# A recurrent layer stack on one core: the channel mix's output product in three passes by block pairs, the second norm by ScalarE, the numerator ahead of the mixing

## The reference, cut to what matters

```
h  = layernorm(x, ln1_w, ln1_b);  hh = time_shift(h)
xk, xv, xr = h * tm + hh * (1 - tm)            # tmk, tmv, tmr
k, v, sr = xk Wk', xv Wv', sigmoid(xr Wr')
x  = x + (sr * wkv(time_decay, time_first, k, v)) Wo'
h  = layernorm(x, ln2_w, ln2_b);  hh = time_shift(h)
xk = h * cmk + hh * (1 - cmk);  xr = h * cmr + hh * (1 - cmr)
kf = square(relu(xk Wck'))                     # 1024 hidden channels
kv = kf Wcv'                                   # "channel mix's output product"
x  = x + sigmoid(xr Wcr') * kv
```

## Time and profile before

| what | value |
|---|---|
| median of three runs | 1927.9 us (1927.41 to 1932.6) |
| the profiled execution | 1932.82 us, its span 1931.1 us |
| mean granted TensorE clock | 0.967 of full |
| TensorE matmul busy | 1812.3 us (94%) |
| TensorE weight load busy | 1536.1 us (80%) |
| VectorE busy | 1233.3 us (64%) |
| ScalarE busy | 841.0 us (44%) |
| GpSimd busy | 2.7 us (0%) |

### The profile page before, as it was taken

The page is one execution under the profiler, slowest core; times in us unless marked ns, Lnnn a source line. Parts: engine busy times, 40 slices in busy tenths (PEclk is TensorE's granted clock), DMA queues, the critical chain, the costliest instruction groups (busy, mean ns, idle before and its releaser), DMA issues. The chain is left out here.

```text
span 1931.1 us, 26354 instructions
## 1 busy us (share of the span) xinstructions
PE 1812.3 (94%) x10124; PEld 1536.1 (80%) x10124; DVE 1233.3 (64%) x1953; ACT 841.0 (44%) x1304; POOL 2.7 (0%) x24
## 2 busy tenths in 40 slices
PE   2499999999999997999899999999999999999997
PEld 1277887777887776777689998899998899998996
DVE  6889999899998844677554454454454454454445
ACT  2565776666766543333233333333333333333333
POOL 0000000000000000000000000000000000000000
PEclk9699999999999998999789999999999999999999
DMA  3000000001001003111020000000000000001001
GB/s 109 6 22 17 12 27 34 6 28 39 1 12 49 1 1 95 42 42 36 11 76 33 34 25 10 33 33 33 33 18 14 33 33 33 33 11 60 1 1 39
DMA packets 35274, 56.54 MB, mean 29 GB/s; under 512 B 3094, under 2 KB 20476, under 8 KB 34684
## 3 DMA queue, kind: packets, MB, share of 16 engines
q1 hardware_dynamic: 35196, 55.47, 8.8%
HBM read 51.79 MB, written 3.67 MB: 29 GB/s over the span
## 5 line engine op out<-in xcount | busy, mean ns | idle before, releaser
L1489 DVE TENSOR_TENSOR hf<-sil,fbanks 128x512 f32<-128x512 f32 (+1 forms) x128 | 79.4, 620 | 332.2 <-PE fbanks L1658 273.4
L1597 ACT ACTIVATE sil<-fbanks 128x512 f32<-128x512 f32 (+1 forms) x128 | 69.6, 544 | 442.2 <-PE fbanks L1658 442.2
L1674 PE MATMUL fbank<-wl,hh 128*128 128x256 f32 x896 | 250.3, 279 | 0.0
L1674 PE MATMUL fbank<-wh,hl 128*128 128x256 f32 x896 | 250.1, 279 | 0.0
L1674 PE MATMUL fbank<-wh,hh 128*128 128x256 f32 x896 | 250.1, 279 | 0.0
L715 PE MATMUL pair<-wcv,kf 128*112 128x256 f32 x768 | 176.2, 379 | 0.0
L1489 DVE TENSOR_TENSOR hf<-sil,fbank 128x512 f32<-128x512 f32 (+1 forms) x128 | 79.5, 621 | 149.7 <-PE fbank L1658 142.7
L1674 PEld LDWEIGHTS fbank<-wl,hh 128*128 128x128 f32 x896 | 168.3, 188 | 2.2
L1674 PEld LDWEIGHTS fbank<-wh,hh 128*128 128x128 f32 x896 | 168.4, 188 | 1.8
L1674 PEld LDWEIGHTS fbank<-wh,hl 128*128 128x128 f32 x896 | 168.4, 188 | 0.0
L1496 DVE TENSOR_TENSOR hl<-hf,hh 128x512 fp32r<-128x512 f32 (+1 forms) x256 | 158.2, 618 | 0.0
(11 more groups left out here) (235 smaller groups left out, 3495.1 us busy)
## 6 DMA issues: line engine op xcount, KB each, us to landing
raw<-in_w_gate SPq DMA_DIRECT2D x16, 512.0 KB, 3.8
raw<-in_w_up SPq DMA_DIRECT2D x16, 512.0 KB, 4.7
raw<-in_w_down SPq DMA_DIRECT2D x16, 512.0 KB, 5.6
raw<-in_w_ck SPq DMA_DIRECT2D x4, 1024.0 KB, 4.8
wcv<-in_w_cv SPq DMA_DIRECT2D x4, 768.0 KB, 4.4
raw<-in_ctx_t SPq DMA_DIRECT2D x4, 750.0 KB, 6.3
ct<-in_ctx_t SPq DMA_DIRECT2D x4, 750.0 KB, 5.1
x<-in_x SPq DMA_DIRECT2D x4, 448.0 KB, 6.1
```

The lines of the kernel that those rows point to most:

```text
L1489: dve.tensor_tensor(hf[i][:, 0:w], sil[i][:, 0:w], bank[2 * i + 1][:, 0:w], ALU.mult).then_inc(hf_ready, 1)
L1597: act.activation(sil[f % 2][:, 0:w], bank[2 * (f % 2)][:, 0:w], ACT.Silu).then_inc(sil_ready, 1)
L1674: ins = pe.matmul(bank[4 + 2 * (t % 2) + i // 2][:, (i % 2) * C:(i % 2 + 1) * C], a[t % 2][:, f, i * P:(i + 1) * P], m[h][:, DOWN + f * C: ...
```

## The change

1. All 8 blocks of the output product are split (`SPLIT` is gone, `FT = 8`), so it has 96 fp32r matmuls a step. The tile `wcv` and its load go; the whole of `in_w_cv` (1024 KB) passes through `stage`, and `wcvh`, `wcvl` have 2048 columns in place of 512.
2. The product runs over block pairs outside and sequences inside, so that four sums (two banks, two sums in each) stay open. TensorE does pairs 0 and 1, the transposes of norm 1, pairs 2 and 3. Each pair waits for its own `kfl_ready`; `cv_done` comes in the last pair.
3. ScalarE copies all four groups of `kf` to `kfh`, VectorE makes four `kfl`, in four places of its list.
4. Norm 2 is done by ScalarE (four `Identity` activations with scale and shift), as norm 1 is; VectorE makes the shift in one small instruction. ScalarE now does norm 1 of step s+2 ahead of `rsqrt0(2, s)`.
5. The numerator moves on VectorE from behind `mix_ck` to ahead of the mixing of norm 1.
6. To make room, `ckl` takes the place of `mix_ck` in memory, `kfl` that of `kf`, and `diff` is `dk`.

```
 VectorE's loop:
                         low_weights(2 * l, wckl, wckh, ck_done, 4 * GROUPS * l)
+                if valid(s - 1):
+                    low_kf(s - 1, 3)
                 if valid(s + 1):
                     wkv_denominator(s + 1)
                 if valid(s):
                     rsqrt(2, s)
-                    normalise(2, xn[2], chunk(s), xn_ready[2])
+                    set_shift(2)
+                if valid(s + 1):
+                    wkv_numerator(s + 1)
                 if valid(s + 2):
                     n = difference(1, s + 2)
                     mix(1, s + 2, ("k", "v", "r"), ("tmk", "tmv", "tmr"), mix1_ready, n)
...
                     mix(2, s, ("ck",), ("cmk",), mix2_ready, n)
-                if valid(s + 1):
-                    wkv_numerator(s + 1)
...
                     low_kf(s, 0)
                 if valid(s + 3):
                     rsqrt(1, s + 3)
-                    set_shift(s + 3)
+                    set_shift(1)
                 if valid(s):
-                    for j in range(1, SPLIT // 2):
-                        low_kf(s, j)
+                    low_kf(s, 1)
                 if valid(s + 2):
                     wkv_sums(s + 2)
+                if valid(s):
+                    low_kf(s, 2)
 ScalarE, hidden() and the loop:
                 act.wait_ge(ck_done, 4 * m + j + 1)
-                split = 2 * j < SPLIT
-                if m and split:
-
-                    act.wait_ge(kfl_ready, SPLIT // 2 * (m - 1) + j + 1)
-                if m and not split:
+                if m and j == 0:
 
                     act.wait_ge(cv_done, 2 * m)
...
-                if not split:
-                    return
                 act.wait_ge(square_done, 4 * m + j + 1)
-                if m and j == 0:
-
-                    act.wait_ge(cv_done, 2 * m)
-                act.activation(kfh[:, 2 * j:2 * j + 2], t[:], ACT.Copy).then_inc(kfh_ready, 1)
+                act.activation(kfh[:, 2 * j:2 * j + 2], t, ACT.Copy).then_inc(kfh_ready, 1)
...
                     wkv_exp(s + 1, 2)
+                if valid(s + 2):
+                    normalise(1, s + 2)
                 if valid(s):
                     rsqrt0(2, s)
-                if valid(s + 2):
-                    normalise1(s + 2)
                 if valid(s + 1):
                     reciprocal0(s + 1)
                 if valid(s + 2):
                     norm_out(1, s + 2, pair[2], "ln1w", "ln1b")
                 if valid(s):
+                    normalise(2, s)
                     norm_out(2, s, pair[0], "ln2w", "ln2b")
 TensorE:
+            def channel_out(m, pairs):
+                for p in pairs:
+                    pe.wait_ge(kfl_ready, FT // 2 * m + p + 1)
+                    for i in range(G):
+                        for f in range(2):
+                            j = 2 * p + f
+                            for n, (a, w) in enumerate(((kfh[:, j], wcvh), (kfh[:, j], wcvl), (kfl[p][:, f], wcvh))):
+                                ins = pe.matmul(pair[3][0:T, i // 2, (i % 2) * C:(i % 2 + 1) * C],
+                                                a[:, i * T:(i + 1) * T], w[:, j * C:(j + 1) * C],
+                                                start=j == n == i % 2 == 0,
+                                                stop=j == FT - 1 and n == 2 and i % 2 == 1)
+                        if i % 2 and p == FT // 2 - 1:
+                            ins.then_inc(cv_done, 1)
...
-                    pe.wait_ge(w_in["cv"], 16 * (m // GROUPS + 1))
-
                     pe.wait_ge(cth_ready, m + 1)
-                    channel_out(m, (0, 1, 2))
+                    channel_out(m, (0, 1))
...
-                    channel_out(m, (3,))
+                    channel_out(m, (2, 3))
 Memory and loads:
-        wcvh, wcvl = sb("wcvh", [P, SPLIT * C], F32R), sb("wcvl", [P, SPLIT * C], F32R)
-        wcv = sb("wcv", [P, (F // P - SPLIT) * C])
+        wcvh, wcvl = sb("wcvh", [P, FT * C], F32R), sb("wcvl", [P, FT * C], F32R)
...
+        diff = dk
...
-                    ("cr", wcr, cr_done, 1), ("cv", wcv, cv_done, 2))
+                    ("cr", wcr, cr_done, 1))
...
-                if name == "cv":
-                    w = w[:, 0:SPLIT * C]
```

More of the change, by code:

```diff
@@ L24 @@
 LN_EXP, EXP_TANH = "natural_log_exp_and_others", "exp_and_others"
-SPLIT = 2
+FT = F // P
 NAMES = ["ln1w", "ln1b", "tmk", "tmv", "tmr", "td", "u", "ln2w", "ln2b", "cmk", "cmr", "w"]
@@ L118, in rwkv_phase @@
         rstd = {k: sb(f"rstd{k}", [T, G]) for k in (0, 1, 2)}
-        shift = sb("shift", [T, G])
+        shift = {k: sb(f"shift{k}", [T, G]) for k in (1, 2)}
         h = {1: sb("h1", [P, CB, G, T1]), 2: sb("h2", [P, CB, G, T1])}
-        diff = sb("diff", [P, CB, G, T])
-        mixed = {n: sb("mix_" + n, [P, CB, G, T]) for n in ("k", "v", "r", "ck", "cr")}
+        mixed = {n: sb("mix_" + n, [P, CB, G, T]) for n in ("k", "v", "r", "cr")}
         kp = sb("kp", [P, CB, G, T1])
@@ L137, in rwkv_phase @@
         bb = sb("bb", [P, CB, G, T1])
-        ckh, ckl = sb("ckh", [P, CB, G * T], F32R), sb("ckl", [P, CB, G * T], F32R)
-        kf = [sb(f"kf{i}", [P, 2, G * T]) for i in range(4)]
-        kfh, kfl = sb("kfh", [P, SPLIT, G * T], F32R), sb("kfl", [P, SPLIT, G * T], F32R)
+        ckh = sb("ckh", [P, CB, G * T], F32R)
+        with nc.sbuf_tensor("mix_ck", [P, CB, G, T], FP32) as t:
+            mixed["ck"] = t
+        ckl = sb("ckl", [P, CB, G * T], F32R)
+        with nc.sbuf_tensor("kf", [P, FT, G * T], FP32) as t:
+            kf = [t[:, 2 * j:2 * j + 2] for j in range(FT // 2)]
+        t = sb("kfl", [P, FT, G * T], F32R)
+        kfl = [t[:, 2 * j:2 * j + 2] for j in range(FT // 2)]
+        kfh = sb("kfh", [P, FT, G * T], F32R)
         cth = sb("cth", [T, G, C])
@@ L148, in rwkv_phase @@
         wexp_done, w_ready = sem("wexp_done"), sem("w_ready")
-        w_in = {n: sem("w_in_" + n) for n in ("k", "v", "r", "o", "cr", "cv")}
+        w_in = {n: sem("w_in_" + n) for n in ("k", "v", "r", "o", "cr")}
         stage_in, whi_ready, wlo_ready = sem("stage_in"), sem("whi_ready"), sem("wlo_ready")
@@ L157, in rwkv_phase @@
         h_ready = {k: sem(f"h_ready{k}") for k in (1, 2)}
-        shift_ready = sem("shift_ready")
+        shift_ready = {k: sem(f"shift_ready{k}") for k in (1, 2)}
         mix1_ready, mix2_ready = sem("mix1_ready"), sem("mix2_ready")
@@ L224, in _ @@
                     w = io["w_" + n][l].rearrange("p b c -> p (b c)")
-                    t = tile if n == "cv" else tile[:].rearrange("p b c -> p (b c)")
-                    sp.dma_start(t[:, :], w[:, -t.shape[1]:]).then_inc(w_in[n], 16)
+                    sp.dma_start(tile[:].rearrange("p b c -> p (b c)"), w).then_inc(w_in[n], 16)
                     if l == 0 and n == "r":
@@ L264, in rsqrt, with normalise, set_shift @@
                 after(did(dve.scalar_tensor_tensor(rstd[k][:], yy[k][:], -3.0 * C, y0[k][:], ALU.add, ALU.mult)))
-            def normalise(k, out, xc, done=None):
+            def normalise(k, xc):
                 for i in range(G):
[L268 to L273, removed]
-                return n
-            def set_shift(m):
-                dve.scalar_tensor_tensor(shift[:], mean[1], -1.0, rstd[1][:], ALU.mult, ALU.mult)\
-                    .then_inc(shift_ready, 1)
+                    n = did(dve.tensor_scalar(xc[:, i, :], xc[:, i, :], mean[k][:, i:i + 1], rstd[k][:, i:i + 1],
+                                              ALU.subtract, ALU.mult))
+                return n
+            def set_shift(k):
+                dve.scalar_tensor_tensor(shift[k][:], mean[k], -1.0, rstd[k][:], ALU.mult, ALU.mult)\
+                    .then_inc(shift_ready[k], 1)
             def first_norm(m):
@@ L286, in first_norm @@
                 rsqrt(0, m)
-                after(normalise(0, xc, xc))
+                after(normalise(0, xc))
                 dve.wait_ge(params_in, 48)
@@ L375, in wkv_out @@
                 dve.wait_ge(rec_ready, m + 1)
+                dve.wait_ge(mix1_ready, 6 * min(m + 2, STEPS))
+                if m:
+                    dve.wait_ge(mix2_ready, 4 * m)
                 after(did(dve.tensor_tensor(tokens(dk), tokens(dp), at(e1b, 1), ALU.mult)))
@@ L396, in low_kf @@
             def low_kf(m, j):
-                dve.wait_ge(kfh_ready, SPLIT // 2 * m + j + 1)
-                dve.tensor_tensor(kfl[:, 2 * j:2 * j + 2], kf[j][:], kfh[:, 2 * j:2 * j + 2], ALU.subtract)\
+                dve.wait_ge(kfh_ready, FT // 2 * m + j + 1)
+                dve.tensor_tensor(kfl[j], kf[j], kfh[:, 2 * j:2 * j + 2], ALU.subtract)\
                     .then_inc(kfl_ready, 1)
@@ L513, in norm_out, with normalise @@
                                    bias=param(m, b, b_), scale=param(m, b, w)).then_inc(h_ready[k], 1)
-            def normalise1(m):
-                act.wait_ge(shift_ready, m + 1)
+            def normalise(k, m):
+                act.wait_ge(shift_ready[k], m + 1)
                 xc = x[:, (m % GROUPS) * G:(m % GROUPS + 1) * G, :]
```

(10 more changed lines are left out.)

## The result

The changed kernel takes 1955.83 us (median of four runs, 1954.94 to 1957.41) where the kernel before takes 1930.25 in the same comparison: ratio 1.0134, 95% interval 1.0113 to 1.0154. It is slower by 26 us. The profiled execution took 1955.98 us, its span is 1954.1.

A forecast was written before the change was run, and what follows sets the result against it. TensorE was taken to bound the kernel, VectorE close behind. Dear passes 4 x 5.2, `wckh` passes 3 x 1.4, ordinary -6 x 0.6, tail -5.3, head +2 gave +18, with clock +24: 1952 us, range 1931 to 1965.

The forecast's parts named there:

- the step on the clock: Granted clock falls behind TensorE's wait ahead of norm-2 transposes in four dear passes: 1.4 us each, bounds 0 to 2.3.
- Head and tail: Pass 0 loses 2 us (bounds 0 and 4); passes 14 to 16 gain 5.3 us together from TensorE's saving.
- TensorE's saving: Output product on TensorE falls from 13.4 to 11.6 us, saving 1.8 a pass; its own list then lasts 38.7.
- An ordinary pass: Pass without weight splits: TensorE waits 1.2 us for norm 1; 39.9 us, 0.6 less than before, six in the sum.
- VectorE's load: VectorE's busy time in a pass rises from 36.95 to 38.8 us, as full as TensorE.
- The dear pass: Pass behind `wcvh` (s = 1, 5, 9, 13): late `wcvh` delays norm 2; 46.7 us against 41.52, +5.2 each.
- The pass with `wckh`: Passes s = 4, 8, 12: copy ahead of `eu` makes TensorE wait 3.0 us for norm 1; 41.9 us, +1.4 each.
- TensorE's floor: Rival, 4%: every pass shrinks by TensorE's 1.8 us, 16 x 1.8 = 29, giving 1899 us.
- the rule that I named: Skill's rule to optimise the highest-occupancy engine first, TensorE by weight-load share; by it TensorE's saving would be the gain.
- VectorE's floor: Rival, 10%: ScalarE's chain is hidden and `wcvh` comes in time; VectorE needs 160.5 us for four passes, giving 1915.
- The rival of better ordinary passes: Rival, 14%: norm 1 isn't late, nine passes gain 1.2 us more and the clock holds; +7, 1935 us.
- The clock fell oftener: Rival, 10%: clock falls of 2.3 us in four dear and three `wckh` passes, 16 instead of 5.6; +34, 1962 us.

The follow-up runs named there:

- e2: Changed kernel with ScalarE's fourth hidden group behind norm 1 of the next step and VectorE's fourth `kfl` behind the denominator; ratio 1.0067 to the kernel before.
- a: Changed kernel with ScalarE's copy to `wcvh` moved from behind the exponentials to behind the copy to `ckh`; 1923.68 us, ratio 0.9972 to the kernel before.
- g: Kernel before, with staging, `wcvh` and `wcvl` of all 2048 columns though the product uses 512; ratio 1.0078 to the kernel before.
- h: The edit of e2 on top of a; 1922.17 us, ratio 0.9963 to the kernel before.
- s: Kernel before with the move of a, its `wcvh` copy (512 columns) behind the copy to `ckh`; 1925.22 us, ratio 0.9980 to the kernel before.
- b: As a, with `wckh`'s copy behind `norm_out` of norm 2, `wckl` behind `low_ck`, and two staging buffers; ratio 0.9982 to the kernel before.
- c: Changed kernel with norm 2 back on VectorE, norm 1's new place on ScalarE kept; ratio 1.0190 to the kernel before.
- p: As b, with the low halves of both weights made by GpSimd; ratio 1.0045 to the kernel before.
- q: As p, with the edit of e2; ratio 1.0041 to the kernel before.

## Why the prediction was right, point by point

- **The forecast** was +24 us on both the profiled execution and the median; measured are +23.2 and +25.6. As a time, 1957 met 1955.98 on the profiled execution, and 1952 met 1955.83 on the median: the step of 4.9 between the two was the kernel before's and did not carry over. That the sum comes so close is in part luck. The clock took 3.8 us more than forecast, while the head took 1.6 less and the attention part, which is not in the sum, 3.3 less.
- **TensorE's saving.** An ordinary pass has 38.70 us of matmul work in it, as forecast (38.7), and lasts 39.89 (39.9), with the wait of 1.19 (1.2) for norm 1. Run e2 took away what I had named as the cause, and the wait went, though VectorE held the pass at 39.66.
- **VectorE's load.** 38.93 in the window (38.8).
- **The dear pass.** 46.42 in place of 46.7. `wcvh` began 10.7 us behind the start of the hidden product (10.7), `add_wkv` 23.5 (23.6), norm 2 ended at 33.2 (33.3). VectorE's wait ahead of `wcvl` was 7.37, outside the 4 to 6 that I had named; nothing in the sum hung on it. The forecast set all four passes against 41.52, but pass 1 of the kernel before took 40.66, which is 0.8 us more of a loss. a shows that the place of the copy decides it: the whole excess goes with it. g shows that on the kernel before its size alone gives 2.9 to 3.5 a pass, some of it by the clock.
- **The pass with `wckh`.** Forecast 41.9, measured 44.50. The wait was right (2.98 for 3.0), and run a's pass 8 took 41.94. What failed is the step on the clock: I had put it in the dear pass, behind the 3.4 us ahead of norm 2, at 1.4 each. That wait was 3.09 to 3.11 in passes 5, 9 and 13, and the clock stayed at 1.00. It fell in pass 1 alone of the dear ones, where it fell twice, behind waits of 2.46 and 3.10, and cost 1.65. And it fell behind the shorter wait of pass 4, 8 and 12, where I had put nothing, and cost 2.6 each time. The term was 5.6 and came out as 9.4.

The changed kernel's windows, ahead of the norm-1 transposes of pass 4 and around the norm-2 transposes of pass 5, and then the row of the same wait in pass 1 with the window behind it:

```profile
262.00:263.00 1.00, 0.00 (x0) 0.00 (x0) 1.00 (x2) 1.00 (x3) 0.00 (x0) 0.88 0.00 0
263.00:264.00 1.00, 0.62 (x4) 0.62 (x5) 1.00 (x2) 0.72 (x3) 0.00 (x0) 0.50 0.36 49
...
319.00:320.00 1.00, 1.00 (x9) 1.00 (x10) 1.00 (x2) 0.36 (x1) 0.00 (x0) 1.00 0.00 0
...
146.64 1.73 PE L659 MATMUL pair<-ident,xn 112*128 112x112 f32 x8 [3.10 <-ACT xn L524]
147.00:148.00 1.00, 1.00 (x8) 1.00 (x7) 1.00 (x3) 0.34 (x1) 0.00 (x0) 0.50 0.00 0
```

- **Head and tail.** The head cost 0.4 up to pass 1 (2 forecast). Passes 14 to 16 gave 5.1 (5.3).
- **What I had not in the sum.** The attention part, from its first projection to the experts' first matmul, took 236.18 us in place of 239.46, at a mean granted clock of 0.90 in place of 0.88. In runs a and h it was 235.58 and 236.36. Its instructions are the same in all of them. The two runs on the kernel before show that the change is not needed for such a difference: the part took 239.38 us in g (clock 0.88) and 233.17 in s (0.91). So the 3.3 us can't be credited to the change. It goes with the clock; what sets the clock there was not tested.
- **The rivals.** TensorE's floor is refuted by the result: matmul busy time fell by 20 us, and the time rose. I had also misapplied the rule that I named for it. The Trainium skill ("Perfetto Trace Analysis", section "Identifying the Most-Contended Engine") calls matmul busy time no good measure for TensorE and judges it by its matmul flops and its weight-load share instead. By the earlier trace rows that share is 32.0 of 40.52 us, 79%, and VectorE's busy share 36.95 of 40.52, 91%, so by that share VectorE was the fuller engine, which agrees with the result. VectorE's floor is what is left once the waits are gone: h's 162.1 for four passes stands 1.6 above the 160.5 that I had worked out, and VectorE's two waits of 0.73 are nearly all of that. The rival of better ordinary passes did not come. The clock fell oftener than forecast, but nearer to my figure (9.4 to 5.6) than to the rival's 16.

In the experiments my own theory failed five times. On b I moved VectorE's work and did not ask what it meets in the next place, on c I followed one chain only, on h I did not see that VectorE was full, and on p and q I had no price for GpSimd's work beside VectorE's.

## What to carry to other kernels

Here the engine that bound, TensorE, had under 10% more to do than the next one, VectorE, and a change that took 4% from the first and gave 5% to the second was paid for in waits. Where two engines are that near, work out each engine's list against the others' for one ordinary period and for the rare one (here a period with weights in it), for the rare one decides. A one-off copy that others wait for belongs where its engine is idle, as early as its own inputs allow; here one move of one line was worth 32 us, 27 of them in the passes at which it was aimed. And after removing a wait, look for the second-latest input of the same instruction.

## What the runs showed of the hardware that I had not expected

- The same wait of TensorE, 2.98 us, was followed by a fall of the granted clock from full to half in pass 4 of run a and not in pass 8, and a wait of 3.09 in the changed kernel's pass 5 was not either, while the same wait in pass 1, 3.10, was. Shorter ones were too: 2.46 in pass 1, and 2.52 in pass 9 of run g, the only wait of that pass. A fall cost 1.2 to 2.6 us of its pass in the passes with `wckh`, and in run a the next pass gave it back. The Trainium skill ("TensorE: Matmul & The Clock Gate", section "What's actually happening") says that activity releases the throttle; the runs agree in the direction, and show that a wait of about 3 us can go both ways.
- A VectorE instruction with two inputs that begins while GpSimd does a two-input operation of 2048 columns can stand until that one is through: 5.37 us in place of 1.09. The Trainium skill ("Perfetto Trace Analysis", section "Optimizing Scalar/DVE Operations") says that the two share a read port and that moving work between them might not help; here p, which differs from b by that move alone, took some 12 us more.
